# The degrees' running sum: GpSimd transfers that add in memory, in place of GpSimd additions and the slices' loads

## The reference, cut to what matters

```python
def _L1_gnn_ref(H, A, mask, W, b):
    A_hat = A + jnp.eye(N, dtype=A.dtype)
    deg = A_hat.sum(axis=-1)
    dis = (deg + EPS) ** (-0.5)
    A_norm = dis[:, :, None] * A_hat * dis[:, None, :]
    H_lin = jnp.einsum('bni,oi->bno', H, W) + b
    out = jnp.einsum('bnm,bmo->bno', A_norm, H_lin)
    ...
x = x + _L0_gnn_ref(_layernorm(x), adj, ...)    # five groups of nodes, two graph convolutions each
x = x + _L0_ffn_ref(_layernorm(x), ...)         # eight experts, the best two for each row
x = x + _L1_gnn_ref(_layernorm(x), adj, nodemask, ...)
x = x + _L1_ffn_ref(_layernorm(x), ...)
```

## Time and profile before

| | |
|---|---|
| median of three runs | 1250.68 us (1248.07 to 1252.08) |
| the profiled execution's own time | 1253.57 us |
| its span in the trace | 1251.8 us |
| granted TensorE clock, mean | 0.938 |
| block one ends, block two begins | about 234.8 us |
| POOL's sixteen additions (L430) | 37.8 us busy, 88.8 to 219.3 us |
| landing of a slice `an` on SP's queue | 3.9 / 4.7 / 8.1 us (least, median, most) |

### The profile page before, as it was taken

The page is one execution under the profiler, slowest core; times in us unless marked ns, Lnnn a source line. Parts: engine busy times, 40 slices in busy tenths (PEclk is TensorE's granted clock), DMA queues, the critical chain, the costliest instruction groups (busy, mean ns, idle before and its releaser), DMA issues. The chain is left out here.

```text
span 1251.8 us, 20777 instructions
## 1 busy us (share of the span) xinstructions
PE 1143.5 (91%) x6346; PEld 856.7 (68%) x6346; DVE 1060.6 (85%) x3170; ACT 949.8 (76%) x1885; POOL 735.5 (59%) x678
## 2 busy tenths in 40 slices
PE   6889979459999999999999981899999999999998
PEld 4667756327788888888888861566667666666675
DVE  4678987897999999999999975688888888888875
ACT  3448765448999999999999971687787877877874
POOL 3346555636666666655666617776677766777720
PEclk9999985559999999999999995899999999999999
DMA  5579764502323333322333542223222232222310
GB/s 196 195 221 293 228 196 143 200 21 74 83 81 76 84 83 85 83 78 79 83 85 85 72 64 70 58 76 85 69 72 73 70 88 72 70 73 72 81 37 26
DMA packets 136466, 124.51 MB, mean 99 GB/s; under 512 B 14591, under 2 KB 116067, under 8 KB 135204
## 3 DMA queue, kind: packets, MB, share of 16 engines
q1 hardware_dynamic: 119075, 87.77, 22.8%
q0 software_dynamic: 17280, 35.42, 13.2%
HBM read 83.64 MB, written 39.50 MB: 98 GB/s over the span
## 5 line engine op out<-in xcount | busy, mean ns | idle before, releaser
L1081 POOL DMA_INDIRECT exg<-xln_scratch,ids x284 | 279.5, 984 | 190.9 <-PE p_ex L1134 105.4
L1380 POOL DMA_INDIRECT yg<-expert_rows_scratch,pos_i x256 | 254.5, 994 | 97.1 <-issue 72.7
L1102 ACT ACTIVATE ehr<-p_eh,bc 128x512 f32<-128x512 f32 x284 | 195.2, 687 | 22.7 <-DVE ehl L1222 19.2
L1222 DVE TENSOR_TENSOR ehl<-ehr,ehh 128x512 fp32r<-128x512 f32 x284 | 191.4, 691 | 7.0 <-ACT ehh L1105 6.8
L1105 ACT ACTIVATE ehh<-ehr 128x512 fp32r<-128x512 f32 x284 | 179.6, 633 | 9.0
L1138 PE MATMUL p_eh<-exh,wh 128*128 128x512 f32 x284 | 124.6, 439 | 0.8 <-ACT exh L1096 0.8
L1150 PE MATMUL p_ey<-ehl,wh 128*128 128x512 f32 x284 | 116.8, 411 | 0.0
L1387 POOL TENSOR_TENSOR root_l<-pre_l,mhalf 128x4 f32<-128x4 f32 x64 | 66.5, 1039 | 80.1 <-DVE pre_l L1654 79.2
L1142 PE MATMUL p_eh<-exl,wh 128*128 128x512 f32 x284 | 112.1, 395 | 0.0
L1139 PE MATMUL p_eh<-exh,wl 128*128 128x512 f32 x284 | 112.0, 394 | 0.0
L1147 PE MATMUL p_ey<-ehh,wh 128*128 128x512 f32 x284 | 112.0, 394 | 0.1
(11 more groups left out here) (226 smaller groups left out, 2912.4 us busy)
## 6 DMA issues: line engine op xcount, KB each, us to landing
expert_rows_scratch<-eyo SPq DMA_DIRECT2D x71, 256.0 KB, 2.3
xtok<-in_x_tok SPq DMA_DIRECT2D x8, 1024.0 KB, 7.3
an<-in_a_t SPq DMA_DIRECT2D x16, 512.0 KB, 4.7
xln_scratch<-xl SPq DMA_DIRECT2D x16, 512.0 KB, 4.4
at<-in_a_t SPq DMA_DIRECT2D x32, 256.0 KB, 3.0
out<-outx SPq DMA_DIRECT2D x32, 256.0 KB, 2.6
wj<-in_w_grp SPq DMA_DIRECT2D x16, 321.0 KB, 4.8
exg<-xln_scratch,ids POOLq DMA_INDIRECT x284, 2.6
```

Source lines behind the costliest of these rows:

```text
L1081: pool.indirect_dma_start(out=xg[p][:, k, :], out_offset=None, in_=xln_d, in_offset=bass.IndirectOffsetOnAxis(ap=ids[:, R * j + k:R * j + ...
L1102: nc.scalar.activation(hr[c % 2][:, :], p_h[c][:, :], ACT.Relu, bias=bc[p][:, c:c + 1])\
L1222: nc.vector.tensor_tensor(hl[:, c, :], hr[c % 2][:, :], hh[:, c, :].bitcast(F32), ALU.subtract)\
L1380: pool.indirect_dma_start(out=yg[p][:, c, k, :], out_offset=None, in_=y_d, in_offset=bass.IndirectOffsetOnAxis(ap=pos_i[:, c, R * j + k:R ...
```

## The change

`degrees(b)` is no longer an addition of POOL. POOL issues a transfer from the adjacency in memory straight onto `dsum`, and the transfer adds (`accum_op=ALU.add`). Each waits until the one before has landed, the first for the zeroing of `dsum`. The wait on `gnb` is gone. SP's sixteen loads into `an` are gone. The three folding additions stay, behind a wait for the sixteenth transfer.

```diff
@@ SP
-                        if 0 <= i + 1 < NB and i + 1 < 2:
-                            load_adjacency(i + 1)
-                        if 2 <= i < NB:
-                            load_adjacency(i)
                         if 2 <= i < NB + 2:
                             store_normalised(i - 2)
@@ POOL
                     def degrees(b):
-                        pool.wait_ge(gnb_ready, b + 1)
-                        pool.wait_ge(an_loaded[b % 2], 16 * (b // 2) + 16)
-                        pool.wait_ge(deg_ready, b + 1)
-                        nc.gpsimd.tensor_tensor(dsum[:, :, :], dsum[:, :, :], an[b % 2][:, :, :], ALU.add)\
-                          .then_inc(deg_ready, 1)
+                        if b == 0:
+                            pool.wait_ge(deg_ready, 1)
+                        else:
+                            pool.wait_ge(an_loaded[0], 16 * b)
+                        pool.dma_start(dsum[:, :, :], a_t.rearrange("m b n -> b m n")[:, RG * b:RG * b + RG, :],
+                                       accum_op=ALU.add).then_inc(an_loaded[0], 16)
...
+                    pool.wait_ge(an_loaded[0], 16 * NB)
                     for k, m in ((1, 4), (2, 2)):
-                        pool.wait_ge(deg_ready, NB + k)
+                        pool.wait_ge(deg_ready, k)
```

More of the change, by code:

```diff
@@ L445, in _ @@
                             roots(b)
+                    pool.wait_ge(an_loaded[0], 16 * NB)
                     for k, m in ((1, 4), (2, 2)):
-                        pool.wait_ge(deg_ready, NB + k)
+                        pool.wait_ge(deg_ready, k)
                         nc.gpsimd.tensor_tensor(dsum[:, 0:m, :], dsum[:, 0:m, :], dsum[:, m:2 * m, :], ALU.add)\
                           .then_inc(deg_ready, 1)
-                    pool.wait_ge(deg_ready, NB + 3)
+                    pool.wait_ge(deg_ready, 3)
                     nc.gpsimd.tensor_tensor(deg[:, :], dsum[:, 0, :], dsum[:, 1, :], ALU.add).then_inc(deg_ready, 1)
-                    pool.wait_ge(deg_ready, NB + 4)
+                    pool.wait_ge(deg_ready, 4)
                 @block.scalar
```

## The result

The changed kernel takes 1256.23 us (median of 7 runs, 1254.34 to 1259.89) against 1251.04 us before (7 runs): a ratio of 1.0035, 95% interval 1.0021 to 1.0048. It is slower, by 0.35% (5.2 us) and not by the 1.2% (14.6 us) that was forecast; the time itself lies in the stated range of 1249 to 1290 us. Timed again later, it came to 1.0031 (1.0019 to 1.0044).

What follows compares the result with a forecast made beforehand. Bound taken: PE, DVE and transfers near their end to 152 us, then DVE, then PE at low clock. +13.8 us (late turns) + 2 (middle) - 1.2 (DVE) = +14.6 on 1250.68, so 1265 us; range 1249 to 1290.

Steps and rivals of the forecast that it cites:

- L: Time from one adding transfer's issue to its landing, claimed as the least length of a turn: 8.9 us.
- what each lacks to 8.9: Late turns: each interval shorter than L is stretched to 8.9 us, summing to 13.8 us.
- term for the addition: Part of L: the transfer also fetches 1024 rows of `dsum` at 38 ns over sixteen engines, 2.4 us.
- fixed part: Part of L: fixed cost and first rows, taken from POOL's indirect gather of 128 rows, 2.6 us from issue to landing.
- company: Part of L: SP's store of `xl` starts together with POOL's transfer and takes 1.8 us of all engines.
- rival C: Late turns: `ct` comes earlier without `an` on SP's queue and the clock stays up, 1242 us; chance 0.07.
- The middle turns: From 98 to 152 us: the slices' added engine time costs 2 us, bounds 0 and 10.
- POOL's issue time: POOL's time to issue a transfer: between 0.98 and 7.9 us, taken under the free 3.9 us, so costing nothing.
- rival B: POOL's issue is the bound: at 7.9 us an issue, about +53 us, 1304 us; chance 0.12.
- The second read: An adding transfer needs two source reads, so half the rate; by that L is 8.9 us, without it 6.5.
- DVE's 1.2 us: Six turns with group work: L658 no longer held up by POOL's addition, 0.2 us each, 1.2 us gained.
- The end of block one: After the last transfer: its 8.9 us landing replaces a 2.36 us addition, using 6.5 of POOL's 10.8 us idle, so hidden.

Runs made afterwards that it cites:

- e11: The changed kernel with only the last nine of the sixteen adding transfers, seven slices of the sum left out: ratio 1.0024 to the kernel before.
- e1: The changed kernel with two running sums taken in turn, so each transfer waits only for the one before the last: ratio 1.0045 to the kernel before.
- e6: The changed kernel with SP's store of `xl` moved behind the loads of `ct`: ratio 1.0012 to the kernel before.
- e2: The changed kernel with POOL's sixteen transfers plain, without adding, the sum left out and the waits the same: ratio 1.0014 to the kernel before.
- e10: The changed kernel with only the first seven of the sixteen adding transfers, nine slices of the sum left out: ratio 0.9996 to the kernel before.
- e9: The changed kernel again, with no edit, timed beside the kernel before: ratio 1.0031.
- the floor: Kernels with no load, addition or transfer of a slice, in either order of `ct` and store on SP: ratios 0.9958 and 0.9971 to the kernel before.
- e12: The changed kernel with a second, plain transfer of the same slice behind each adding one, into a buffer nobody reads: ratio 1.0131 to the kernel before.
- e4: The kernel before with SP's sixteen loads but without POOL's additions, the sum left out: ratio 0.9994 to the kernel before.
- e8: The kernel before with two slices loaded once and POOL's sixteen additions kept, fourteen loads left out: ratio 0.9996 to the kernel before.
- e3: No load, addition or transfer of the slices, the degrees' sum left out: ratio 0.9958 to the kernel before.
- e5: The kernel before with SP's store of `xl` moved behind the loads of `ct`: ratio 0.9997 to the kernel before.

## Why the prediction was wrong, step by step

**The step that failed** is "from the first to the last transfer no turn can be shorter than L", with the price "what each lacks to 8.9", 13.8 us. Two things were off.

The size: L was put at 8.9 us, and it is 7.4 as a median of all sixteen and 6.7 in the late turns, where the price was taken. The term for the addition was about right: 65 ns a row, against the twice 38 assumed. What was too much is the rest. A fixed part of 2.6 us was added in front of the moving; in e11's 6.5 us, POOL's issue of 1.6 and the moving of 4.2 leave 0.7. The 1.8 us for company were added whole, and in the late turns next to none of them shows; it is in the middle that landing takes 8.5 us. By the prediction's own price the late intervals lack 2.0 us to 6.7 and 4.5 us to 7.4, so that most of the 13.8 was size.

The rule itself, and that is the mistake in the mechanism: a wait of POOL was priced as if it shifted everything behind it. The distances between two issues are at least the landing time, as forecast (6.8 to 8.6 us in the late turns). But POOL idles 2.7 to 5.4 us in front of `groot` in every late turn, for DVE or ACT and never for its own transfer, and the only interval of `groot` as short as 5.9 us has longer ones beside it, so that a late issue is caught up. The earlier trace rows had that idle time (2.99 us), and the prediction even named it. In the changed kernel POOL has six waits of an issue for a landing, 4.5 us in all. e1 takes them away and gains nothing; e6 multiplies them and is not slower. Thus the 13.8 us were about zero.

So it would have been luck had the sum come out. With the measured 7.4 us it would have read 4.5 + 2 - 1.2 = 5.3 us, beside the measured 5.2, out of a term that e1 shows to be about nothing. And the sign that the prediction set for itself, a landing of 7 to 10 us, was met by the median and did not test the rule.

**What costs instead** is most likely the engines' time, through other transfers; how much of it by which is in part open. Shown: the adding takes 4.2 us of the engines instead of 1.8 and costs some 0.2 to 0.3% beyond the same transfer without it (e2); moving `ct` ahead of the store gives about 0.2% back and takes PE's wait at `p_sel` away (e6), though its trace is shorter in the middle turns too; the nine late transfers cost more than the seven of the middle (e10, e11). Not shown is that the wait at `p_sel` is what those 0.2% are. The idle gap at `p_sel` was in rival C, which looked only at the 1.8 us that leave SP's queue. The transfers with 4.2 us came in by the other queue at the same time.

**The middle turns**, forecast at +2 us of bounds 0 to 10: from the first `groot` to the seventh the changed kernel's trace shows +1.4 us (63.72 against 62.29), its second trace (e9) +4.1 (66.37). e10 is 0.25 to 0.4% over the floor, 3 to 5 us, where the kernel before pays a part of that too. Roughly right, near the lower bound, as taken. The extra is not spread evenly: the changed kernel has one interval of 12.9 us, 128.15 to 141.07, where before the longest is 11.72. SP's issue of `wj`, in front of `ct` in its queue, is held up there, first before, then after:

```profile
126.64 1.69 SPq L378 DMA_DIRECT2D wj<-in_w_grp  x1
```

```profile
126.15 4.37 SPq L374 DMA_DIRECT2D wj<-in_w_grp  x1
```

Intervals of 12.8 us and more are in the traces of e1, e9, e10 and e12 too, all with the adding transfers in the middle, and not in that of e6. In e6, where `wj` too stands ahead of the store, no issue of it from 84 to 150 us takes over 0.97 us. What the long intervals wait for was not isolated.

**POOL's issue time**, "under 3.9 us, and so nothing": 1.58 us, right; rival B was out. 1024 plain rows take 0.92 us (e2), no more than the gather's 0.98, and the adding ones 0.66 us more. By the rule on descriptors cited in the prediction (the Trainium skill, DMA: Bandwidth & Descriptors, "Anatomy of one DMA — SWDGE (gpsimd) path") many of them come before the extra cost shows. For the plain transfer this case's traces agree; with the adding one the extra cost shows.

**The second read**: the Trainium skill, Collectives: The Full Stack, "The bandwidth ceiling: the fold count and why AG ≠ RS ≠ AR", says of ReduceScatter that its add needs two source reads and so halves the rate. Here it is 4.2 us against 1.8, a factor of 2.4; the trace agrees in kind and shows somewhat more. The read itself stands in no row.

**DVE's 1.2 us** of L658: the median went from 408 to 170 ns in six turns (it is L656 in the changed kernel), 1.4 us. The mechanism was right. That it shortens the kernel is not shown (e4: 0.9994, interval 0.998 to 1.0007).

**The end of block one**: POOL's idle time before block two fell from 10.78 to 6.95 us; the last landing is hidden, as said. Block two was to begin 13 to 17 us later, and began 2.1 later.

**What stays open.** The loads alone (e4) and the additions alone (e8) each bring the kernel from the floor of 0.996 to 0.997 to within 0.1% of 1, and both together bring it no further. Costs that don't add up may lie in the late turns, most of which last 5.8 us or 8: the trace of e8 has intervals of 5.92, 5.90, 7.14, 5.90, 7.94 and 8.06 us, one long turn more than e3. What sets which turn is long was not isolated (e3 shows that the clock within the turn is not enough), and it is open why e5 gives nothing though its `p_sel` waits 1.0 us instead of 2.9. These are single traces, and the timed runs of one kernel scatter by 3 to 9 us. No version that still computes the whole sum beat the kernel before: e5 stands at 0.9997, and with the sum left out altogether the gain is only 0.3 to 0.4%. Open too are the 0.2% between e2 and e4, and e12, which cost three times what the engines' time alone had led to expect.

## What to carry to other kernels

An addition in a transfer frees an engine, but here it cost the DMA engines more than twice the time of the plain load it replaced (4.2 against 1.8 us): look first whether the engine was the bound (here POOL was not) and whether the DMA engines have that time. Price a new wait only after subtracting the idle time behind it on the same engine, turn by turn; the waits here, 4.5 us and even 16.8 in e6, cost nothing that could be measured. Then ask which small transfer queued nearby feeds the engine that does set the pace, and try it ahead of the large ones; here that gave 0.2% in the changed kernel and nothing in the one before.

## What the hardware showed that was not expected

- A row of 512 bytes costs 65 ns of a DMA engine when it is added in SBUF, and 28 when it is only written (e2); POOL's issue for 1024 rows is 1.58 and 0.92 us.
- In POOL's plain transfer, 8.39 MB go in 2304 packets of 3.6 KB (e2), in the adding one in 16,640 of 504 bytes. The packets of a plain transfer hold several rows, those of an adding one hold one.
- Removing either of two parts gives nothing and removing both gives 0.3 to 0.4%: e4, e8 and e3.
